# Masking later keys in the second attention pass on GpSimd instead of TensorE

## What is computed

```python
scores = jnp.einsum('bhid,bhjd->bhij', Qh, Kh) / jnp.sqrt(jnp.asarray(Dh, dtype=x.dtype))
causal = jnp.tril(jnp.ones((S, S), dtype=x.dtype))
scores = scores * causal - NEG_BIG * (1.0 - causal)
attn = jax.nn.softmax(scores, axis=-1)
vals = jnp.einsum('bhij,bhjd->bhid', attn, Vh)
```

## Time and profile before

| | us |
|---|---|
| median of three runs | 1136.26 (1133.39 to 1139.63) |
| the profiled execution, time | 1130.96 |
| its span, first to last instruction | 1129.0 |
| mean granted TensorE clock | 0.897 of full |

### The profile page before, as it was taken

The page is one execution under the profiler, slowest core; times in us unless marked ns, Lnnn a source line. Parts: engine busy times, 40 slices in busy tenths (PEclk is TensorE's granted clock), DMA queues, the critical chain, the costliest instruction groups (busy, mean ns, idle before and its releaser), DMA issues.

```text
span 1129.0 us, 25558 instructions
## 1 busy us (share of the span) xinstructions
PE 907.8 (80%) x9800; PEld 472.7 (42%) x9800; DVE 766.4 (68%) x1289; ACT 665.7 (59%) x1448; POOL 310.1 (27%) x573
## 2 busy tenths in 40 slices
PE   2599999953883899998999999508949579999698
PEld 1123232231881445553332322308826345555355
DVE  4789899543543887789898995424456477888355
ACT  2288888830761477777888888306712238777521
POOL 4652310115341223532413101153410122311100
PEclk8599999985895799999999999758969779999989
DMA  6112131271203221112011000012010122110000
GB/s 181 43 35 59 46 99 23 52 69 52 73 33 93 58 60 37 45 41 54 26 40 39 21 3 2 1 38 76 30 40 0 47 63 58 36 35 4 3 10 28
DMA packets 77260, 49.36 MB, mean 44 GB/s; under 512 B 22242, under 2 KB 74754, under 8 KB 77154
## 3 DMA queue, kind: packets, MB, share of 16 engines
q1 hardware_dynamic: 72024, 40.42, 14.9%
q0 software_dynamic: 2496, 5.13, 1.2%
q10 hardware_dynamic: 2634, 2.36, 0.8%
HBM read 12.72 MB, written 9.21 MB: 19 GB/s over the span
## 4 chain that ended last, share of the span: by engine, by line
PE 56%; ACT 13%; issue 11%; DVE 11%; POOL 5%; DMA 3%; ACTq 1%; SPq 1%; DVEq 0%; POOLq 0%
PE ps L601 14%; PE ps L677 13%; ACT pt L737 10%; PE ps L1394 5%; PE ps L1112 4%; PE ps L1121 4%; PE ps L633 3%; DVE negm L847 3%; DVE blockm L838 3%; POOL sorted L1331 3%; PE ps L1382 3%; PE ps L607 3%; PE ps L695 2%; PE ps L637 1%; PE ps L685 1%
## 5 line engine op out<-in xcount | busy, mean ns | idle before, releaser
L737 ACT ACTIVATE pt<-ps 128x512 f32<-128x512 f32 (+1 forms) x896 | 457.4, 566 | 132.0 <-PE ps L601 85.4
L847 DVE TENSOR_REDUCE negm<-ps 128x2 f32<-128x1024 f32 x256 | 301.6, 1220 | 28.4 <-PE ps L601 26.3
L677 PE MATMUL ps<-pt,va 128*32 128x256 f32 (+1 forms) x4352 | 273.3, 340 | 16.3 <-ACT ot L743 7.3
L838 DVE TENSOR_REDUCE blockm<-ps 128x8 f32<-128x1024 f32 (+1 forms) x192 | 195.7, 1043 | 53.3 <-PE ps L601 26.3
L601 PE MATMUL ps<-ks,qs 61*128 61x128 bf16 (+2 forms) x1536 | 175.7, 297 | 31.3 <-DMA ks<-parts 12.0
L601 PE MATMUL ps<-qs,ks 64*128 64x128 bf16 (+3 forms) x1408 | 167.5, 295 | 9.6 <-ACT pt L737 3.2
L677 PEld LDWEIGHTS ps<-pt,va 128*32 128x32 f32 x4352 | 92.0, 108 | 125.0 <-issue 74.2
L601 PEld LDWEIGHTS ps<-ks,qs 61*128 61x128 bf16 x1536 | 56.2, 97 | 186.8 <-issue 99.7
L989 POOL CAST mpart<-negm 128x16 bf16<-128x16 f32 x64 | 13.0, 204 | 331.7 <-PE ps L601 128.1
L1285 DVE COPY pt<-experts 128x1156 f32 x50 | 38.8, 776 | 70.3 <-DVE upd L1296 36.8
L601 PEld LDWEIGHTS ps<-qs,ks 64*128 64x128 bf16 x1408 | 58.1, 94 | 66.7 <-ACT pt L737 47.3
(11 more groups left out here) (161 smaller groups left out, 1121.3 us busy)
## 6 DMA issues: line engine op xcount, KB each, us to landing
qs<-parts SPq DMA_DIRECT2D x80, 128.0 KB
ks<-parts SPq DMA_DIRECT2D x65, 128.0 KB
experts<-in_L_ffn_w SPq DMA_DIRECT2D x16, 256.0 KB
pt<-sorted SPq DMA_DIRECT2D x2, 1225.5 KB, 6.7
sorted<-pad_row SPq DMA_DIRECT2D x6, 384.0 KB, 8.3
qs<-mrow SPq DMA_DIRECT2D x128, 6.0 KB
pt<-y_rows SPq DMA_DIRECT2D x8, 256.0 KB, 3.8
ks<-parts ACTq DMA_DIRECT2D x15, 128.0 KB
```

The costliest lines, as they stand in the source:

```text
L677: ins = pe.matmul(pv_bank[32 * j:32 * j + 32, q0:q1], va[n % 2][:, kb, 4 * g + j, 0 if odd else DH + 1:VW - DH - 1 if odd else VW], pt[:, ...
L737: a.activation(pt[:, k_ % NPT, S * s:S * s + width], b_bank(o + s)[:, 0:width], ACT.Exp).then_inc(b_free, 1)
L838: v.tensor_reduce(blockm[:, g % 2, :, t, PLACES[c_]], pair_of(ka)[:, :, 0:width].rearrange("p s (b c) -> p s b c", c=P), AX, ALU.max, nega ...
L847: v.tensor_reduce(negm[:, g % 2, :, t, c_], pair_of(ka), AX, ALU.max, negate=True).then_inc(a_free, 1)
```

## The change

In pass 2 of causal batches the score products carry no mask products. After the exponentials of a diagonal step, GpSimd sets the probabilities of later keys to zero in place in `pt`, with an index select over 128 partitions by 8 blocks of 128 (1024 elements a partition). It does so at the place of the `p2` event in its list, and `pv` of piece 0 waits for a new semaphore. Pass 1 keeps its masks; `mask_k` is still built.

```diff
+        later_keys_out = sem("later_keys_out")
...
+        at_diagonal = {}
...
                 if name == "p2":
                     at_step[ev] = len(at_step)
+                    if causal_of[ev[1]] and ev[2][1] == 0:
+                        at_diagonal[ev] = len(at_diagonal)
...
-                    ends = score_pieces(pe, PASS2[w["causal"]][c_], w["causal"] and c_ == 0,
-                                        [b_bank(o), b_bank(o + 1)],
+                    ends = score_pieces(pe, PASS2[w["causal"]][c_], False, [b_bank(o), b_bank(o + 1)],
                                         [ks[n % NQK][rows[s], 2 * g + t, :] for s in range(2)],
-                                        [qs[n % NQK][rows[s], 2 * g + t, :] for s in range(2)], mask_k)
+                                        [qs[n % NQK][rows[s], 2 * g + t, :] for s in range(2)], None)
...
                     need(pe, b_free, at_b[("p2", n, (g, c_, 1))] + 2)
+                    if w["causal"] and c_ == 0:
+                        need(pe, later_keys_out, at_diagonal[("p2", n, (g, 0, 1))] + 1)
...
+                elif ev in at_diagonal:
+
+                    need(g_, b_free, at_b[ev] + 2)
+                    step_ = pt[:, at_step[ev] % NPT, :].rearrange("p (i c) -> p i c", c=P)
+                    g_.affine_select(out=step_, in_=step_, compare_op=ALU.is_ge, fill=0.0, base=0,
+                                     pattern=[[0, 2 * TB], [1, P]], channel_multiplier=-1).then_inc(later_keys_out, 1)
```

## The result

| | before | after |
|---|---|---|
| median, us (lowest to highest, runs) | 1134.83 (1130.67 to 1139.63, 4) | 1149.85 (1147.30 to 1151.53, 4) |
| span of the profiled execution | 1129.0 | 1149.8 |

What follows compares the result with a forecast made beforehand. TensorE was taken to set the pace in program order. Masks saved and waits at `pv` added summed to +16.0 us, less 1 for later waits: 1136.3 + 15 = 1151 us, 8 in 10 for 1139 to 1168.

Steps and rivals of the forecast that it cites:

- The select: One `affine_select` of 128x1024 f32 on GpSimd, 64 in all, was taken to last 1.11 us.
- Quads 2 of preparing batches: Six quads with `qlo` ahead of and `klo` between the selects: `pv` later, +2.0 us each, +12.0 together.
- Quads 3: Six quads where `pv` would wait for the second select: +0.56 us each, +3.4 together.
- the 1 us: Taken off the sum because TensorE's later waits in a quad would partly make up for the stall.
- Quads 0: Among eight even quads where `pv` would wait for the second select: +0.26 us each, +2.1 together.
- quads 1: Six long quads of preparing batches, select hidden behind projections, so only the masks' saving counts: -0.44 us each, -2.6 together.
- The masks: 256 `mask_k` matmuls out of pass 2, 0.22 us a diagonal step, all on a TensorE-bound path: 14.1 us saved.
- The granted clock: Rival, chance 0.05: TensorE's new stalls let the throttle lower the clock in the causal stretches, up to +20 us more, 1171.
- the ends: Four quads at the ends of the two causal stretches: +0.8 us for the last, +0.2 each for three, +1.4 together.
- absorbed: Rival, chance 0.13: select at its lower bound and TensorE's later waits shrink by their full length: +4 us, 1141.
- Faster: Rival, chance 0.07: the second select is done before TensorE reaches `pv`, so only the masks' 14.1 us count: 1122.
- The slow select: Rival, chance 0.08: a GpSimd select of 1.3 us or more, +26 to +78 us, 1162 to 1214.

Runs made afterwards that it cites:

- e2: The kernel before with its pass 2 mask products kept and the selects added: 1159.40 us, ratio 1.0234 to before.
- e8: The changed kernel with each select over the first head's four blocks only: 1135.08 us, ratio 1.0030 to before.
- e7: The changed kernel with `qlo` and `klo` behind the selects and `pv` of causal batches one step later: 1125.59 us, ratio 0.9955 to before.
- e3: The changed kernel with `qlo` and `klo` moved behind both selects of quad 2: 1138.99 us, ratio 1.0050 to before.
- e1: The changed kernel without the selects, so neither masks in pass 2 nor selects: 1120.78 us, ratio 0.9915 to before.
- e11: e3 with the selects of quads 0 left out: 1136.05 us, ratio 1.0028 to before.
- e5: The changed kernel with `pv` of causal batches one step later, `qlo` and `klo` left in place: 1134.85 us, ratio 1.0020 to before.
- e10: The kernel before with `qlo` and `klo` later and `pv` one step later in quads 2 and 3 alone: 1135.52 us, ratio 1.0033 to before.
- e12: e3 with the selects of quads 3 left out: 1136.46 us, ratio 1.0000 to before.

## Why the prediction was right, point by point

Forecast 1151, measured 1149.85, slower as said. The mechanism is shown from both sides: e2 adds the selects alone and is 27 us slower, e8 halves them and gives 12 to 15 back, e7 hides them and all of the loss is gone. The size is partly right by luck; term by term, with the quads 3 that have a lowered clock in after taken from e3:

- **The select, 1.11 us**: 1.09. Both the rate and the handoffs were right: in quad 3 of batch 6 from the first step's last exp (494.61) to `pv` (496.95) 2.34 us, predicted 2.36.
- **Quads 2 of preparing batches, +2.0**: +1.80, with `klo` between the selects as said (e3: most of it goes when they are moved). From the start of `qlo` (443.46) to `pv` (447.89) it took 4.43 us, where the prediction's terms add up to 4.61: three of the four operations start 0.03 to 0.04 us before the one ahead ends. Of the six (batch 7's is +2.08), +11.1 for +12.0.
- **Quads 3, +0.56**: +0.38, six of them +2.3 for +3.4. TensorE waits 0.92 us where the sum has 1.00, and its busy time fell by 0.54 (7.91 to 7.37), 0.10 more than the masks. Its other idle time in the quad stayed (0.11, then 0.10), so the 1 us that the prediction took off for later waits made good is not seen here. Why the busy time fell further is open.
- **Quads 0, +0.26, and quads 1, -0.44**: together -0.18, measured -0.49, but by another mechanism. The prediction treated TensorE's 12.91 of 13.14 busy us as proof that TensorE led. It did not throughout: e1 takes 0.88 us of masks out of the two quads and they give 0.46; e11 takes the wait out and they give 0.1. The chain of waits of the kernel before, with VectorE on it from 456.96 to 463.02, would have told this.
- **The masks, 14.1 us**: 10.0 in e1's stretches. The 0.22 a step is right; that "all of it" is on the path failed in the six long quads and in two of batch 7.
- **The granted clock** stood as a rival with a chance of 0.05 and up to 20 us. It came, at 8.4 us in the profiled execution. The forecast's sum without it should have been 11.2, not 16 (quads 2 0.9 too high, quads 3 1.1, the other even quads 0.9, quads 1 0.8, the ends 1.1, of which two lie outside the stretches); the two errors cancelled. The base of the forecast was 1136.3, the median of three executions; later medians lie 4 us lower. That the stalls bring the lowered clock is likely, not shown. Of the six quads 3 right behind a stall of 2.5 us (2.3 in e2), five have it in after and two in e2; in the other twelve traces, where TensorE never waits over 1.6 us for GpSimd at `pv`, none of the 72 quads 3 in the same places has it. But pieces elsewhere came without them: in the last batch of e5, e10, e11 and e12 as well, and e10 has no select at all.

The rivals: "absorbed" did not come. The select was not at its lower bound, and TensorE's idle time outside the new wait did not shrink: in quads 2 it was 0.6 us before, without the wait for the evacuation, and 0.6 after (10.18 less 7.09 and 2.49). "Faster" was out, since a select would need to take 0.6 us. The slow select was out at 1.09.

The 1.8 cycles an element of the Trainium skill (GPSIMD Engine Reference, "Side-by-side cycle accounting") would give this operation an estimated 1.54 us; the trace disagrees with that figure, at 1.09. The same section of the Trainium skill gives 1.03 cycles an element for the shortest loop bodies; the trace's 0.89 ns an element is 1.07 cycles at 1.2 GHz, near that one.

## What to carry to other kernels

An idle engine is not a free one: what is moved to it costs the latency of its own queue, so look at what stands ahead of and between the moved instructions there (here `klo`, 1.1 us, six times) and at how many steps lie between producer and consumer. Move the consumer and the queue's neighbours together with the work; the same change that lost 15 us gains 5 to 7 with both moved (e7). And cut the stretch into its periods and read the chain of waits in each: 98% busy on one engine did not mean that this engine led.

## What the runs showed of the hardware

An index select on GpSimd over 128 partitions took 1092 ns for 1024 f32 and 636 ns for 512 (e8), in place, with rows of 128: 0.89 ns for each further element and some 180 ns fixed. With the fixed part it is 1.07 ns an element, against 0.88 for a memset of 2048 f32, which reads nothing (1806 ns), and 2.26 for a two-input operation on 512 f32 (1159 ns).

70 us of selects on GpSimd left the others' instructions as long as they were: 1220 ns for VectorE's maxima over 128x1024, 597 ns for ScalarE's exps of 128x512.

In the kernel with stalls of 2.5 us the granted clock fell to 1.2 GHz six times for a few us inside the causal stretches, and a quad then took 1.4 us longer. In the profiled execution of the kernel before it stayed at full speed there throughout. That the stalls are the cause is not shown.
